# Attention scores made once and kept in SBUF, with a running maximum in place of a pass of its own for the maximum

## The chip, the core and the metric

The kernel runs on one core of a Trainium2 chip. The metric is the device time of one execution in microseconds (us). The core's engines are called as the profile calls them: PE is TensorE, which multiplies matrices (PEld its loading of weights), DVE is VectorE, ACT is ScalarE, POOL is GpSimd, SP is SyncE. PE writes to PSUM only; the other engines here read PSUM or SBUF and write SBUF, and POOL works in SBUF alone.

## What is computed

One decoder layer over x of 32 x 56 x 128: a small LSTM with Gaussian attention weights, then cross-attention to a context of 32 x 1500 x 128 with 16 heads, then a feed-forward stage with 4 experts. The part that the change touches is the cross-attention:

```
q = (Q @ WQ).reshape(N, ql, HEADS, DK)
k = (K @ WK).reshape(N, kl, HEADS, DK)
v = (V @ WV).reshape(N, kl, HEADS, DV)
compat = jnp.einsum('nqhk,nlhk->nhql', q, k) / math.sqrt(DK)
weights = jax.nn.softmax(compat, axis=3)
attn = jnp.einsum('nhqk,nkhv->nqhv', weights, v).reshape(N, ql, HEADS * DV)
return attn @ WO + bO
```

Q is the normalised x, K and V are both the context.

## The kernel before

The weights are folded ahead, WQ with WK and WV with WO, so that per batch element there is one query matrix of 128 x 896 (16 heads x 56 positions), the context itself as key and as value, and one projection per head. The 32 batch elements ("batches") are worked on in 16 pairs. On each engine a function `period(i, k)` writes out one batch, b = 2i + k, as 12 slots; `sequence` writes the first pair, a loop over the middle pairs and the last pair. Nothing but this written order and the semaphores (`need`) sets what runs when.

The context of a batch is cut into 12 chunks of 125 rows. For each chunk:

* **Scores** (PE, `scores`): 125 x 896, in two halves of 448 columns. Context and query are each held as a high and a low part in the type float32r (`ctxT_hi`, `ctxT_lo`, `q_hi`, `q_lo`), and three matmuls per half give hi*hi + hi*lo + lo*hi. Scores go to one of two double banks of PSUM (`score_ps`).
* **Exponential** (ACT, `probs`): reads `score_ps`, writes one of four buffers `probs`.
* **Weighing** (PE, `weigh`): the chunk of the context (`ctx_nat`) times the probabilities, in plain f32, two matmuls of 448 columns (two records each in the profile), summed over the 12 chunks in the PSUM banks `usum_ps`.
* **Sum** (POOL): `prob_sum` += the chunk, 11 additions per batch.

The softmax needs the maximum first. Before a batch's scores are made, PE makes an approximate product the other way round (`side("max")`, 21 matmuls of q_hi x ctxT_hi into 128 x 500), DVE reduces each (`read_max`), builds a diagonal matrix (`max_diag`), PE spreads it over all partitions with two matmuls by ones (`side("spread")`), ACT copies the negative to `neg_max` and ACT writes it into `score_ps` ahead of every chunk (`seed`); the score matmuls add on top of it. All this is done for batch b + 1 beside the work on batch b.

Further work stands in the slots by letters in the table `PLACES` (four places in each slot): t turns a third of the context of batch b + 2 (PE transposes, ACT `turned_hi`, DVE `turned_lo`), q makes a quarter of the next pair's queries (PE, ACT `stage_query`; then ACT `query_hi`, DVE `query_lo`), s takes the sums and p the projections of the pair before (DVE `invert_sums`, `add_heads`). They share two PSUM banks, `SIDE` and `SIDE + 1`: a piece may start once the piece before it in its bank has been read. In the last pair the tokens for the feed-forward stage are normalised, and the experts chosen (`choose_experts`). The feed-forward stage follows, beginning at `hidden(0, 0)`.

Of the kernel before, what the change touches and what calls it, by code (L numbers as in the profile page):

```python
# [18 lines left out]
F32R = mybir.dt.float32r  # L19
# [6 lines left out]
def decoder_layer(nc, x, ctx_1024, W_ih, W_hh, b_ih, b_hh, W_mu, b_mu, W_sig, b_sig,  # L26
# [8 lines left out]
    TOK = 2 * S  # L35
# [17 lines left out]
    NP = 4  # L53
    assert CR * CH == L and RB * 128 == HQ and PAIRS % G4 == 0 and S % U8 == 0

    with ExitStack() as stack:
# [15 lines left out]
        ones_r = sb("ones_r", [128, 128], F32R)  # L72
# [38 lines left out]
        def cut(size, parts=128):  # L111
# [4 lines left out]
        neg_max = [cut(HQ).rearrange("p (a b) -> p a b", a=2) for n in range(2)]  # L116
        cut(3 * HQ)
# [3 lines left out]
        first_sum = q_stage[0:CR, 0]  # L121
# [67 lines left out]
        xT_halves = max_diag[:].rearrange("p (n t) -> p n t", n=2)  # L189
# [6 lines left out]
            "ln_step ln_var rstd_done ln_done xT_ps xT_sb ones_r_made "  # L196
# [5 lines left out]
            "max_ps max_read max_found diag_done spread_ps neg_done seeded scored prob_done "  # L202
# [18 lines left out]
        PLACES = ("m..m mssm ssmm mmpm .mpm mmpm mmpm mqmm mqqt ..dd qt.. t...",  # L221
                  "m..m mm.m mm.m mm.m m.m. m.m. m.mt m.m. m.mt ..dd .... .t..")
# [1308 lines left out]
```

## Time and profile before

| | |
|---|---|
| median of the runs shown | 1717.54 us (1717.15 to 1722.96) |
| the profiled execution | 1721.62 us |
| span of its profile | 1719.5 us |
| LSTM, self-attention, first queries | 0 to 158 us |
| maximum of batch 0 | 158 to 177.6 us |
| cross-attention, 32 batches | 177.6 to 1615.3 us |
| feed-forward stage | 1615.3 to 1719.5 us |
| busy: PE, ACT, DVE, POOL | 96%, 53%, 49%, 46% |

The 14 pairs of the loop repeat each 89.6 us. Records of matmuls overlap, since they are pipelined, so their durations add up to more than the time; what a matmul costs is read from start to start. Durations of the other engines reach about 0.1 us past the start of the next instruction on the same engine for the same reason.

### The profile page before, as it was taken

The page shows a single profiled execution, that of the slowest core. Times are in us where ns is not written, and L with a number is a line of the kernel's source. Part 1 is how long each engine was busy: PE and PEld are TensorE (multiplying, and loading weights), DVE is VectorE, ACT ScalarE, POOL GpSimd, SP SyncE. Part 2 cuts the span into 40 slices and gives each one's busy share as a digit, 9 for nine tenths or more (in the row PEclk, how much of TensorE's full clock was granted, in tenths as well). Part 3 has the DMA queues.
Part 4 walks back from the last instruction along what each step waited for, and adds up shares of the span by engine and source line. Part 5 has one row for each costly group of instructions (what it writes and reads, how often), then busy time and mean ns, then how long its engine had stood idle before and what let it go on. Part 6 is the DMA issues. An engine that isn't in the chain of part 4 may idle for free.

```text
span 1719.5 us, 25064 instructions
## 1 busy us (share of the span) xinstructions
PE 1647.4 (96%) x7783; PEld 1181.7 (69%) x7783; DVE 843.5 (49%) x1772; ACT 918.7 (53%) x1311; POOL 792.1 (46%) x414
## 2 busy tenths in 40 slices
PE   6876999999999999999999999999999999998997
PEld 3344677777777777777777777767677777776664
DVE  3349445454545444454545445454454545454345
ACT  3233565656565656555555556565656565655211
POOL 2003454545454555545455555454545454545410
PEclk9996899999999999999999999999999999999788
DMA  4000000000000000001010101000000000000000
GB/s 150 25 17 2 1 36 37 36 36 36 36 36 36 36 36 36 36 29 43 18 45 15 44 20 40 31 36 36 36 36 36 36 36 36 36 18 1 1 1 22
DMA packets 15052, 54.84 MB, mean 32 GB/s; under 512 B 919, under 2 KB 6122, under 8 KB 15022
## 3 DMA queue, kind: packets, MB, share of 16 engines
q1 hardware_dynamic: 15022, 54.46, 8.4%
q8 instruction: 17, 0.28, 0.1%
q14 instruction: 13, 0.11, 0.0%
HBM read 53.54 MB, written 0.92 MB: 32 GB/s over the span
## 4 chain that ended last, share of the span: by engine, by line
PE 87%; DVE 8%; ACT 2%; issue 1%; POOL 1%; DMA 0%; DVEq 0%; POOLq 0%; ACTq 0%
PE ps L729 32%; PE ps L717 26%; PE ps L598 9%; PE ps L617 3%; PE ps L629 3%; PE ps L779 3%; PE ps L609 3%; PE ps L590 2%; DVE max_diag L1259 2%; PE ps L524 1%; DVE max_parts L1252 1%; PE ps L603 1%; DVE xnorm L1099 1%; ACT arena L877 1%; ACT arena L880 1%
## 5 line engine op out<-in xcount | busy, mean ns | idle before, releaser
L452 POOL TENSOR_TENSOR arena<-arena,probs 125x896 f32<-125x896 f32 x320 | 677.6, 2118 | 546.8 <-ACT probs L1033 456.6
L729 PE MATMUL ps<-probs,ctx_nat 125*128 125x448 f32 x1536 | 685.7, 544 | 0.0
L1252 DVE TENSOR_REDUCE max_parts<-ps 128x1 f32<-128x500 f32 x672 | 451.6, 676 | 354.7 <-PE ps L598 347.2
L1033 ACT ACTIVATE probs<-ps 125x896 f32<-125x896 f32 x384 | 351.6, 916 | 474.3 <-PE ps L717 430.9
L598 PE MATMUL ps<-ctxT_hi,q_hi 128*128 128x500 f32 x672 | 365.1, 544 | 2.2 <-DVE max_parts L1252 1.3
L976 ACT ACTIVATE ps<-arena 125x896 f32<-125x896 f32 x384 | 354.1, 922 | 7.9
L729 PEld LDWEIGHTS ps<-probs,ctx_nat 125*128 125x128 f32 x1536 | 277.6, 191 | 95.8 <-issue 79.7
L717 PE MATMUL ps<-q_hi,ctxT_hi 128*125 128x448 f32 x768 | 331.2, 431 | 1.8 <-ACT ps L976 1.8
L717 PE MATMUL ps<-q_lo,ctxT_hi 128*125 128x448 f32 x768 | 282.8, 368 | 0.0
L717 PE MATMUL ps<-q_hi,ctxT_lo 128*125 128x448 f32 x768 | 281.7, 367 | 0.0
L717 PEld LDWEIGHTS ps<-q_hi,ctxT_hi 128*125 128x125 f32 x768 | 144.5, 188 | 70.0 <-issue 62.1
L598 PEld LDWEIGHTS ps<-ctxT_hi,q_hi 128*128 128x128 f32 x672 | 127.4, 190 | 82.2 <-DVE max_parts L1252 29.7
L717 PEld LDWEIGHTS ps<-q_lo,ctxT_hi 128*125 128x125 f32 x768 | 144.2, 188 | 42.5 <-issue 22.1
L717 PEld LDWEIGHTS ps<-q_hi,ctxT_lo 128*125 128x125 f32 x768 | 143.2, 186 | 14.2
L447 POOL TENSOR_TENSOR arena<-probs 125x896 f32<-125x896 f32 x32 | 68.4, 2139 | 149.0 <-ACT probs L1033 149.0
L1139 DVE TENSOR_TENSOR ctxT_lo<-ps,ctxT_hi 128x500 fp32r<-128x500 f32 x96 | 64.4, 670 | 131.0 <-ACT ctxT_hi L898 131.0
L1244 DVE TENSOR_TENSOR q_lo<-arena,q_hi 128x896 fp32r<-128x896 f32 x32 | 38.8, 1212 | 92.8 <-ACT q_hi L963 92.8
L898 ACT ACTIVATE ctxT_hi<-ps 128x500 fp32r<-128x500 f32 x96 | 56.3, 587 | 45.9 <-PE ps L590 45.9
L617 PEld LDWEIGHTS ps<-vo_w,arena 128*112 128x112 f32 x512 | 64.0, 176 | 23.8 <-issue 23.8
L1290 DVE SCALAR_TENSOR_TENSOR resid<-ps,sum_recip,resid 112x128 f32 (+1 forms) x128 | 44.3, 346 | 63.6 <-PE ps L617 63.6
L629 PEld LDWEIGHTS ps<-xT,qk_w 128*128 128x128 f32 x512 | 67.1, 196 | 11.0 <-issue 9.1
L629 PE MATMUL ps<-xT,qk_w 128*128 (+1 forms) x512 | 69.3, 281 | 0.6 <-ACT xT L859 0.6
(186 smaller groups left out, 1259.6 us busy)
## 6 DMA issues: line engine op xcount, KB each, us to landing
ctx_raw<-in_ctx_dram SPq DMA_DIRECT2D x32, 750.0 KB
ctx_nat<-in_ctx_dram SPq DMA_DIRECT2D x32, 750.0 KB
w_sb<-in_L_ffn_W_dram SPq DMA_DIRECT2D x1, 1024.0 KB
resid<-in_x_dram SPq DMA_DIRECT2D x1, 896.0 KB, 6.7
out_dram<-ctx_raw SPq DMA_DIRECT2D x4, 224.0 KB, 2.5
ctx_raw<-in_L_xattn_WQ_dram SPq DMA_DIRECT2D x1, 512.0 KB
w_sb<-in_L_xattn_WK_dram SPq DMA_DIRECT2D x1, 512.0 KB
w_sb<-in_L_xattn_WV_dram SPq DMA_DIRECT2D x1, 512.0 KB
```

The source lines that it names most:

```text
L447: g.tensor_tensor(first_sum if k == 0 else summed, chunk[0], chunk[1], ALU.add).then_inc(s["prob_added"], 1)
L452: g.tensor_tensor(summed, first_sum if j == 2 and k == 0 else summed, chunk[j % NP], ALU.add).then_inc(s["prob_added"], 1)
L598: mm(ps[:, bank, 0:MC], q_hi[nk][:, block_ * 128:(block_ + 1) * 128], ctxT_hi[nk][:, part * MC:(part + 1) * MC], start=True, stop=True).th ...
L617: m = mm(ps[0:TOK, bank, n * D:(n + 1) * D], u_sum[:, h].rearrange("p b q -> p (b q)"), vo_w[:, h, :], start=True, stop=True)
L629: m = mm(ps[:, bank, n * TOK:(n + 1) * TOK], qk_w[:, 4 * which + n, :], xT[:, bass.ds(i + 1, 1), :].rearrange("p k t -> p (k t)"), start=T ...
L717: m = mm(score_ps[j % 2][:, half, :], cx[k][:, rows], q[k][:, cols], start=False, stop=True, skip_group_check=True)
L729: m = mm(usum_ps[:, half, :], ctx_nat[k][:, j, :], probs[j % NP][:, half, :], start=(j == 0), stop=(j == CH - 1))
L898: a(ctxT_hi[k][:, which * MC:(which + 1) * MC], ps[:, bank, 0:MC], ACT.Copy).then_inc(s["ctxT_hi_done"], 1)
L976: a(score_ps[j % 2], neg_max[k][0:CR], ACT.Copy).then_inc(s["seeded"], 1)
L1033: a(probs[j % NP][:], score_ps[j % 2], ACT.Exp, scale=SCALE).then_inc(s["prob_done"], 1)
L1139: v.tensor_tensor(ctxT_lo[k][:, part], ps[:, bank, 0:MC], ctxT_hi[k][:, part].bitcast(F32), ALU.subtract).then_inc(s["ctxT_lo_done"], 1)
L1252: v.tensor_reduce(max_parts[:, which:which + 1], ps[:, bank, 0:MC], AX.X, ALU.max).then_inc(s["max_read"], 1)
```

## The change

The score matmuls of batch b + 1 now run beside the weighing of batch b. Each chunk of scores is copied out of PSUM by ACT (`keep_scores`) into one of 12 buffers `ring`, and DVE keeps an elementwise maximum over the chunks in `run_max` (`run_maximum`, 11 per batch, each waiting for its chunk; ACT's copy of a chunk waits for the maximum that reads it). When all 12 chunks are there, PE turns `run_max` (`turn_max`, 8 transposes), DVE reduces it over the context (`find_max`), and PE spreads the maximum over the partitions (`spread_max`, 8 small matmuls) into the two side banks. DVE then subtracts it from each chunk in place (`subtract_max`), ACT takes the exponential in place (`exponential`; chunk 0 in two halves), and POOL and PE use the same buffer. Gone are the 21 matmuls and reductions, the diagonal, the spreading by ones, the negative maximum and the 12 seeds. The copy of chunk j of batch b + 1 into `ring[j]` waits for `weigh` and for POOL's addition of chunk j of batch b. The side banks hold the maximum until the last subtraction, so that the pieces t, q, s, p start in slot 6. The queries are made two pairs ahead, and the LSTM, self-attention and feed-forward stages stay as they were, but for the last pair's tokens, now mostly one period earlier.

```diff
-        probs = [sb(f"probs{n}", [CR, 2, HALF]) for n in range(NP)]
+        ring = [cut(HQ, CR).rearrange("p (a b) -> p a b", a=2) for n in range(5)]
...
+        run_max = cut(HQ, CR).rearrange("p (a b) -> p a b", a=2)
+        ring.append(wo_raw[0:CR].rearrange("p f n -> p (f n)")[:, 0:HQ].rearrange("p (a b) -> p a b", a=2))
+        ring += [sb(f"ring{n}", [CR, 2, HALF])[:] for n in range(len(ring), CH)]
...
-        PLACES = ("m..m mssm ssmm mmpm .mpm mmpm mmpm mqmm mqqt ..dd qt.. t...",
-                  "m..m mm.m mm.m mm.m m.m. m.m. m.mt m.m. m.mt ..dd .... .t..")
+        PLACES = (".... .... .... .... .... .... .t.t .t.p .p.p .p.. .... ....",
+                  ".... .... .... .... .... .... .t.t .t.q .q.q .qss ss.. ....")
...
+        EARLY = 4
+        SUBS_AT = {1: (4, 5), 2: (6,), 3: (7, 8), 4: (9,), 5: (10, 11)}
+        EXPS_AT = {0: (2, 3), **SUBS_AT}
...
@@ PE
+                    need(pe, "copied", CH * b + j - 1)
+                    need(pe, "maxed", (CH - 1) * (b - 1) + CH - 2 + j if j < 2 else (CH - 1) * b + j - 2)
...
+            for j in range(CH):
+                for half in range(2):
+                    scores(0, 0, j, half)
...
+                for half in range(2):
+                    turn_max(i, k, half)
+                if not last:
+                    for half in range(2):
+                        scores(b + 1, 1 - k, 0, half)
+                for half in range(2):
+                    spread_max(b, half)
+                if not last:
+                    for half in range(2):
+                        scores(b + 1, 1 - k, 1, half)
                 for j in range(CH):
                     for half in range(2):
+                        weigh(i, b, k, j, half)
                         beside(j, half)
                     for half in range(2):
+                        if 1 <= j < CH - 1 and not last:
+                            scores(b + 1, 1 - k, j + 1, half)
                         beside(j, 2 + half)
...
@@ ACT
+            def keep_scores(b, j):
+
+                need(act, "scored", CH * b + j + 1)
+                need(act, "maxed", (CH - 1) * b + j if j else 0)
+                need(act, "weighted", CH * (b - 1) + j + 1)
+                need(act, "prob_added", (CH - 1) * (b - 1) + max(j, 1))
+                a(ring[j], score_ps[j % 2], ACT.Copy).then_inc(s["copied"], 1)
...
+                if not first:
+                    take_u(i, k)
+                exponential(b, 0)
+                exponential(b, 1)
                 for j in range(CH):
+                    if j:
+                        side_copies(i, k, j - 1)
+                    if not last:
+                        keep_scores(b + 1, j)
+                    for n in EXPS_AT.get(j, ()):
+                        exponential(b, n)
+                    if j == 6 and not (isinstance(i, int) and i == PAIRS - 1):
+                        query_hi(i + 1, k)
...
@@ DVE
+            def run_maximum(b, j):
...
+                v.tensor_tensor(run_max, ring[0] if j == 1 else run_max, score_ps[j % 2], ALU.max).then_inc(s["maxed"], 1)
...
+                    v.tensor_tensor(ring[j][:, part], ring[j][:, part], ps[0:CR, SIDE + part.start:SIDE + part.stop, 0:HALF],
+                                    ALU.subtract).then_inc(s["subbed"], 1)
...
+                for half in range(2):
+                    find_max(b, half)
+                if not first:
+                    take_u(i, k)
+                for j in range(EARLY):
+                    subtract_max(b, j)
+                for j in range(1, CH):
+                    if not (last_pair and k == 1):
+                        run_maximum(b + 1, j)
+                    for n in SUBS_AT.get(j, ()):
+                        subtract_max(b, n)
+                    late_turns(i, k, j - 1)
+                    if j == 6 and not last_pair:
+                        query_lo(i + 1, k)
+                    if last_pair:
+                        beside_last_pair(k, j)
+                    side_reads(i, k, j, range(4))
```

**DVE, a whole period (the first, k = 0; the loop repeats it).** Before: `L1252` is the reduction of the maximum, `L1259` the diagonal, `L1139` the low part of the turned context, `L1244` `query_lo`, `L1267` `take_u`.

```order
L1252 TENSOR_REDUCE max_parts<-ps 128x1 [waits s_max_ps] x20
L1256 TENSOR_REDUCE max_all<-max_parts 128x7 [waits s_diag_done,s_max_read]
L1259 TENSOR_TENSOR max_diag<-ident,max_all 128x896 [waits s_spread_ps,s_max_found]
L1139 TENSOR_TENSOR ctxT_lo<-ps,ctxT_hi 128x500 [waits s_ctxT_hi_done] x2
L1244 TENSOR_TENSOR q_lo<-arena,q_hi 128x896 [waits s_q_hi_done]
```

Now, from the end of one period's reads on into the next (its line numbers are the changed kernel's: `L1270` `find_max`, `L1286` `take_u`, `L1278` a subtraction, `L1264` the running maximum, `L1253` `query_lo`, `L1148` the low part of the turned context):

```order
L1270 TENSOR_REDUCE max_all<-ps 112x4 [waits s_spread_ps,s_run_turned] x2
L1286 COPY arena<-ps 128x8x56 [waits s_weighted]
L1278 TENSOR_TENSOR arena<-arena,ps 125x448 [waits s_spread_ps,s_copied]
L1278 TENSOR_TENSOR arena<-arena,ps 125x448 [waits s_spread_ps]
L1278 TENSOR_TENSOR arena<-arena,ps 125x896 [waits s_spread_ps,s_copied] x3
L1264 TENSOR_TENSOR arena<-arena,ps 125x896 [waits s_run_turned,s_copied,s_scored]
L1278 TENSOR_TENSOR arena<-arena,ps 125x896 [waits s_spread_ps,s_copied]
L1278 TENSOR_TENSOR wo_raw<-wo_raw,ps 125x896 [waits s_spread_ps,s_copied]
L1264 TENSOR_TENSOR arena<-arena,ps 125x896 [waits s_maxed,s_scored]
...
L1253 TENSOR_TENSOR q_lo<-arena,q_hi 128x896 [waits s_q_hi_done]
L1264 TENSOR_TENSOR arena<-arena,ps 125x896 [waits s_maxed,s_scored]
L1148 TENSOR_TENSOR ctxT_lo<-ps,ctxT_hi 128x500 [waits s_ctxT_hi_done] x2
```

Twenty-one short reductions have given way to 11 maxima and 12 subtractions over 896 columns, and `query_lo` and the low parts of the context now stand behind them in DVE's order.

**PE, where one batch passes to the next.** Before, between two chunks (`L717` scores, `L729` weighing, `L598` maximum):

```order
L729 MATMUL ps<-probs,ctx_nat 128x448 [waits s_prob_done]
L729 MATMUL ps<-probs,ctx_nat 128x448
L598 MATMUL ps<-ctxT_hi,q_hi 128x500 [waits s_max_read]
L717 MATMUL ps<-q_hi,ctxT_hi 125x448 [waits s_seeded]
L717 MATMUL ps<-q_lo,ctxT_hi 125x448
L717 MATMUL ps<-q_hi,ctxT_lo 125x448
L598 MATMUL ps<-ctxT_hi,q_hi 128x500 [waits s_max_read]
```

Now (`L703` scores, `L717` `turn_max`, `L725` `spread_max`, `L737` weighing):

```order
L717 MATMUL ps<-ident,arena 112x125 [waits s_ctxT_lo_done]
L717 MATMUL ps<-ident,arena 112x125 x3
L703 MATMUL ps<-q_hi,ctxT_hi 125x448 [waits s_copied,s_maxed,s_ctxT_lo_done,s_q_lo_done]
...
L725 MATMUL ps<-ident_r,max_all 125x112 [waits s_max_found]
L725 MATMUL ps<-ident_r,max_all 125x112 x3
L725 MATMUL ps<-ident_r,max_all 125x112 [waits s_max_found]
L725 MATMUL ps<-ident_r,max_all 125x112 x3
L703 MATMUL ps<-q_hi,ctxT_hi 125x448 [waits s_maxed,s_copied]
...
L737 MATMUL ps<-arena,ctx_nat 128x448 [waits s_nat_in1,s_prob_done,s_u_dve,s_u_act]
L737 MATMUL ps<-arena,ctx_nat 128x448 [waits s_prob_done] x2
```

Only two chunks of scores stand between the running maximum and the first weighing that depends on it.

**ACT, the first copies and exponentials of a period, now** (`L987` `keep_scores`, `L993` `exponential`):

```order
L993 ACTIVATE arena<-arena 125x896 [waits s_subbed]
L987 ACTIVATE arena<-ps 125x896 [waits s_prob_added,s_weighted,s_scored]
L993 ACTIVATE arena<-arena 125x896 [waits s_subbed] x2
L987 ACTIVATE arena<-ps 125x896 [waits s_weighted,s_prob_added,s_maxed,s_scored]
L993 ACTIVATE arena<-arena 125x896 [waits s_subbed]
L993 ACTIVATE wo_raw<-wo_raw 125x896 [waits s_subbed]
```

The copy of the next batch's chunk 0 stands ahead of the exponentials of chunks 2 and 3, and waits for POOL.

## Rows read from the trace of the kernel before

**Rows 1.** The page, part 1: busy us, share of the span and instructions by engine.

```profile
PE 1647.4 (96%) x7783; PEld 1181.7 (69%) x7783; DVE 843.5 (49%) x1772; ACT 918.7 (53%) x1311; POOL 792.1 (46%) x414
```

**Rows 2.** Stretches: length, busy us by engine (count), PE clock share, DMA share, GB/s.

```profile
158.00:177.00 19.00, 14.88 (x29) 6.45 (x27) 16.41 (x25) 3.05 (x6) 4.93 (x1) 0.68 0.00 0
880.40:970.00 89.60, 89.34 (x408) 65.68 (x407) 44.13 (x78) 52.94 (x67) 46.57 (x23) 1.00 0.09 34
1555.70:1615.30 59.60, 50.60 (x190) 32.92 (x189) 24.70 (x47) 27.51 (x35) 37.68 (x22) 0.89 0.00 1
1615.30:1719.50 104.20, 93.46 (x369) 64.76 (x368) 46.58 (x127) 13.35 (x23) 12.63 (x12) 0.84 0.04 9
```

**Rows 3.** PE in order of time: chunks without side work (start, us, what).

```profile
1556.95 1.67 PE L729 MATMUL ps<-probs,ctx_nat 125*128 125x448 f32 x4
...
1559.06 0.37 PE L717 MATMUL ps<-q_hi,ctxT_hi 128*125 128x448 f32 x1
1559.27 0.36 PE L717 MATMUL ps<-q_lo,ctxT_hi 128*125 128x448 f32 x1
...
1562.39 1.67 PE L729 MATMUL ps<-probs,ctx_nat 125*128 125x448 f32 x4
```

**Rows 4.** PE in order of time: a maximum, sums, a projection, turns of the context.

```profile
889.88 0.39 PE L598 MATMUL ps<-ctxT_hi,q_hi 128*128 128x500 f32 x1
890.11 0.36 PE L717 MATMUL ps<-q_hi,ctxT_hi 128*125 128x448 f32 x1
...
893.89 0.86 PE L609 MATMUL ps<-ones,arena 125*112 125x1 f32 x8
894.60 1.00 PE L729 MATMUL ps<-probs,ctx_nat 125*128 125x448 f32 x2
...
904.42 1.04 PE L617 MATMUL ps<-vo_w,arena 128*112 128x128 f32 x8
905.30 0.92 PE L729 MATMUL ps<-probs,ctx_nat 125*128 125x448 f32 x2
...
933.81 0.59 PE L590 MATMUL ps<-ident,ctx_raw 125*128 125x125 f32 x4
934.24 1.67 PE L729 MATMUL ps<-probs,ctx_nat 125*128 125x448 f32 x4
```

**Rows 5.** Instructions grouped by line: busy us, mean ns, idle before them.

```profile
L1252 DVE TENSOR_REDUCE max_parts<-ps 128x1 f32<-128x500 f32 x672 | 451.6, 676 | 354.7 <-PE ps L598 347.2 <-issue 6.2
L1033 ACT ACTIVATE probs<-ps 125x896 f32<-125x896 f32 x384 | 351.6, 916 | 474.3 <-PE ps L717 430.9 <-POOL arena L452 37.7 <-POOL arena L447 5.5
L963 ACT ACTIVATE q_hi<-arena 128x896 fp32r<-128x896 f32 x32 | 30.4, 949 | 0.0
L1139 DVE TENSOR_TENSOR ctxT_lo<-ps,ctxT_hi 128x500 fp32r<-128x500 f32 x96 | 64.4, 670 | 131.0 <-ACT ctxT_hi L898 131.0
```

**Rows 6.** DVE and POOL in order of time: operands in PSUM and in SBUF beside POOL.

```profile
1652.12 5.01 POOL L473 TENSOR_TENSOR resid<-resid,arena 112x512 f32<-112x512 f32 x4 [4.39 <-DVE arena L1481]
...
1654.60 1.09 DVE L1342 TENSOR_TENSOR q_lo<-max_diag,ps 128x896 fp32r<-128x896 f32 x1 [2.56 <-PE ps L581]
...
925.45 1.09 DVE L1259 TENSOR_TENSOR max_diag<-ident,max_all 128x896 fp32r<-128x896 f32 x1
...
879.80 2.21 DVE L1259 TENSOR_TENSOR max_diag<-ident,max_all 128x896 fp32r<-128x896 f32 x1
878.95 2.10 POOL L452 TENSOR_TENSOR arena<-arena,probs 125x896 f32<-125x896 f32 x1 [1.33 <-ACT probs L1033]
900.17 4.29 POOL L452 TENSOR_TENSOR arena<-arena,probs 125x896 f32<-125x896 f32 x2 [5.88 <-PE ps L609]
```

**Rows 7.** DVE in order of time: the last pair's token scaling and choice of experts.

```profile
1566.71 6.43 DVE L1099 TENSOR_SCALAR xnorm<-resid,meanvar,rstd 112x128 f32<-112x128 f32 x8 [0.58 <-POOL rstd L377]
...
1594.10 0.20 DVE L1308 TENSOR_REDUCE arena<-arena 112x12 f32<-112x48 f32 x1
...
1602.53 0.61 DVE L1327 TENSOR_TENSOR max_diag<-xT,max_diag 128x448 fp32r<-128x448 f32 x1
```

More of the change, by code:

```diff
@@ L581, in spread_mask, with turn, sums @@
                 mm(ps[:, mask_bank(e), 0:GT], pick_e[:, e, :], onehotT[n], start=True, stop=True).then_inc(s["mask_ps"], 1)
+            def turn(i, k, which, bank):
+                if which == 0:
+                    need(pe, f"ctx_in{k}", 16 * (i + 2))
+                for c in range(TG):
+                    m = tr(ps[:, bank, c * CR:(c + 1) * CR], ctx_in[k][:, which * TG + c, :], ident[0:CR, 0:CR])
+                m.then_inc(s["ctxT_ps"], 1)
+            def sums(pair, which, bank):
+                if which == 0:
+                    need(pe, "prob_added", (CH - 1) * 2 * (pair + 1))
+                for n in range(4):
+                    m = mm(ps[0:TOK, bank, n:n + 1], prob_sum[:, 4 * which + n].rearrange("p b q -> p (b q)"), ones[0:CR, 0:1], start=True, stop=True)
+                m.then_inc(s["sums_ps"], 1)
@@ L619, in side @@
+                    turn(i, k, which, bank)
+                elif what == "sums":
+                    sums(i, which, bank)
+                elif what == "project":
+                    project(i - 1, which, bank)
+                elif what == "query":
+                    query(i + 2, which, bank)
                 elif what == "tokens":
@@ L626, in side @@
                     spread_mask(0, which)
-                elif what == "query":
-                    for n in range(4):
-                        m = mm(ps[:, bank, n * TOK:(n + 1) * TOK], qk_w[:, 4 * which + n, :],
-                               xT[:, bass.ds(i + 1, 1), :].rearrange("p k t -> p (k t)"), start=True, stop=True)
-                    m.then_inc(s["q_ps"], 1)
             def beside_first(u):
@@ L978, in _, with exponential @@
+            def exponential(b, j):
+                for part in ((slice(0, 1), slice(1, 2)) if j == 0 else (slice(0, 2),)):
+                    need(act, "subbed", step_count(b, j, part.stop - 1))
+                    a(ring[j][:, part], ring[j][:, part], ACT.Exp, scale=SCALE).then_inc(s["prob_done"], 1)
             copy_tokens(TOKEN_BANKS[1], 2, 0)
             for u in range(4):
-                stage_query(-1, u, SIDE + u % 2)
-            query_hi(-1, 0)
+                stage_query(0, u, SIDE + u % 2)
```

353 lines of the change are left out of this document (139 added, 214 removed).

## The prediction, made before the changed kernel was run

> **What bounds the kernel now.** The busy shares come first [rows 1]: PE 96%, no other engine over 53%. A share over the whole span says little of a stage, so the stretches come next [rows 2]: in a pair of the loop, 89.60 us long, PE is busy for 89.34. That could still be a PE that works at somebody's pace, so its work is priced from start to start. A chunk of scores and weighing alone takes 2.72 us (1556.95 to 1562.39 is two) [rows 3]. A maximum takes 0.23, a set of four sums 0.71, a set of four projections 0.88, four turns 0.43 [rows 4]. I take the queries, the same eight records of 128 rows, as a projection. A pair then needs 24 x 2.72 = 65.3 for chunks, 42 x 0.23 = 9.7 for the maximum, 4 x 0.71 + 4 x 0.88 + 4 x 0.88 + 6 x 0.43 = 12.5 for side work and about 0.9 for four spreadings by ones. That is 88.4 of 89.6: PE is the bound in the loop, with 1.2 of gaps. ACT and DVE wait for PE there [rows 5]. The ends differ: ahead of the loop PE is granted 0.68 of its clock on average, between its two levels of 1.2 and 2.4 GHz, and follows DVE's reductions, and the last batch takes 59.6 us because PE waits for tokens and for the choice of experts [rows 2].
>
> **What goes from PE.** Per pair the maximum and the spreading, 9.7 + 0.9 = 10.6. New are 16 turns of the running maximum, at 0.105 each as the turns of the context (0.43 for four) [rows 4], 1.7, and 16 small spreadings. The trace has none of 112 columns in float32r; the nearest rows are 0.09 (eight sums in 0.71) and 0.11 (eight projections in 0.88) [rows 4]. I take 0.10, 1.6 in all. The sixteen cost between 0.8, if they ran at half of that, and 3 if at twice. PE's own work falls to 88.4 - 10.6 + 3.3 = 81.1. If PE stayed the bound with the gaps of before, a pair would take 82.3 and the kernel lose some 110 us. So the question is what is late now.
>
> **What the other engines get.** A subtraction or running maximum reads PSUM and SBUF, 896 columns. The row of that form is 1.09 us, and it ran while POOL was busy [rows 6]; with no wait the next instruction starts about 0.08 earlier, so 1.01 apart. DVE per pair: 22 maxima and 24 subtractions, 46 x 1.01 = 46.5, in place of 42 x 0.6. It has room on average (about 65 of 89), as has ACT, whose copies and exponentials replace exponentials and seeds one for one (0.92 from PSUM, 0.95 from SBUF, 0.85 apart) [rows 5]. POOL keeps its 22 additions, 2.19 apart when back to back (two in 4.29, the second of them 2.10) [rows 6]. No engine is full. But each works in its written order, and there are two places where a chain of them is longer than what PE has in hand.
>
> **The first places, at a batch's start.** Let `turn_max` start at 0. PE: turns to 0.84, scores of chunk 0 (six matmuls 0.205 apart [rows 3], 1.23) to 2.07, spreading to 2.5 and 2.9, scores of chunk 1 to 4.1, weighing of chunk 0 to 5.6. DVE meanwhile: two reductions of 500 columns (0.68 each [rows 5]) to 1.9, `take_u` to 2.4, then from 2.7, when the first spreading has landed, half a subtraction, half, and that of chunk 1, done 4.9. Its exponential is done at 5.9; the handover adds 0.1, and PE, ready at 5.6, waits **0.4**. The next wait is longer. Scores of chunk 2 need their PSUM bank, and ACT's copy of the chunk in it goes to `ring[0]`, which POOL must have added: POOL starts at 6.0 with the exponential of chunk 1, ends at 8.2, the copy ends at 9.1, and PE, ready at 7.5, goes on at 9.25: **1.75**.
>
> **The third, in slot 7.** From 9.15 on DVE has 13 instructions ahead of the running maximum of chunk 6 (five maxima, eight subtractions): 9.15 + 13 x 1.01 = 22.3, done 23.4. Behind it in a row: ACT's copy to 24.3, `query_hi` to 25.2, DVE's `query_lo` to 26.3, the maximum of chunk 7 (1.0), the low part of the first turned third (0.67 [rows 5]), done 28.0. PE has six chunks and two groups of turns, 6 x 2.72 + 2 x 0.43 = 17.2, from 9.25 to 26.45, and then wants the side bank of that third: it waits **1.5**. With k = 0 there is a fourth: the second set of projections needs the bank of the last third, whose low part stands on DVE behind the reading of the first set: four additions of heads (1.1), a maximum (1.0) and itself (0.7), 2.8 to 3.0 with the handovers, against PE's weighing of 1.5: **1.5**.
>
> A pair: 81.1 + 2 x (0.4 + 1.75 + 1.5) + 1.5 = **89.9** us, as before. What PE gave away comes back as four waits.
>
> **The whole.** Before the loop: scoring batch 0 runs at DVE's and ACT's pace. The copy of a chunk waits for its maximum and PE for the copy of two chunks earlier: 1.23, 0.16 from the start of the next matmul to the end of a record of 0.36, 1.09 and 0.92, with handovers 3.6 per two chunks, 21.5 for twelve; the clock is at 0.68 there before [rows 2], so I add 2.5. From 159 the first `turn_max` comes at 183, 5.4 later than the first scores did at 177.6. The first pair has no projections and fewer waits: 85. Then 14 pairs of 89.9 less 2 for queries that pair 14 needn't make: 1256.6. Batch 30 takes over the tokens; two scalings took 6.43 beside POOL [rows 7], three cost DVE about 9: 49. The last batch has no scores to make: 5.6 to the second weighing, and 11 x 1.5. But the choice of experts, 8.4 us before (1594.10 to 1602.53) [rows 7], can start only behind the subtractions at 18 and meets a POOL that is never idle: 28 to 29. Two and a half chunks and the one-hot turns follow, partly at the lower clock: 37. The sum is 183 + 85 + 1256.6 + 49 + 37 = 1610.6, where the feed-forward stage began at 1615.3; it keeps its 104.2 [rows 2]. The span becomes 1714.8, less than 1719.5 by 4.7. The profiled execution was 1721.6, 4.1 over the median of the runs. I set the change against the median: 1717.5 - 4.7 = **1713 us**. My own bounds: gaps of 0 to 2.4 in a pair, dear or cheap spreadings and the ends make it 1690 to 1740.
>
> **Rival 1: `query_lo` just misses POOL's gap, slower.** Its two inputs lie in SBUF. Such an instruction took 1.09 with POOL idle and 2.21 when it started 1.25 us before the end of an addition (879.80 against 878.95 + 2.10) [rows 6]: it waits for the end. The Trainium skill (GPSIMD Engine Reference, Key points) says the two engines share SBUF interfaces, with contention when DVE has two SBUF inputs. The trace agrees, and adds that the wait is for the whole rest. In the new period POOL never pauses. By my times it starts its eighth addition 14.1 after the copy at 9.1, if the first at 1.0, and ends at 16.3; `query_lo` arrives at 16.1. It gets in. If the chain of 13 on DVE is 0.3 later, it waits 2.1 more, each batch: 31 x 2.2 = 68, so **1781**. It decides in 2% of the chain.
>
> **Rival 2: DVE's operations come 1.1 apart, slower.** Each now carries two or three waits; 1.01 is from sequences with one. At 1.10 the third wait grows by 15 x 0.09 = 1.35 a batch, 42 us: **1755**.
>
> **Rival 3: the waits aren't there, faster.** If the copies start earlier than I think (POOL's first addition 1 us sooner, handovers hidden), the second and third waits shrink by 1 each: 31 x 2 = 62, **1651**; without any of the four, 1600. For it: the chains exceed PE's work by 1.5 of 17 only. Against it: each wait is written in the code, and their parts have rows.
>
> **A rule that speaks another way.** The Trainium skill (VectorE: DVE Perf Modes, the errata table) gives 120 + columns cycles for a source in PSUM and 58 + columns from SBUF at 0.96 GHz. By an estimate from that page the new operations would take 1.06 us; the row says 1.09, and by the page the third wait would be 0.4 shorter, 12 us less in all. The row decides.
>
> **Chances.** The forecast's case (89 to 91.5 a pair) 0.50; rival 1, 0.15; rival 2, 0.13; rival 3, 0.22, half of it between 1640 and 1690 and half under 1640. About two in ten lie outside 1640 to 1782: that half, and what is worse than rival 1. A difference under 0.5% (1709 to 1726) a measurement hardly tells from none. The forecast's own range of 1690 to 1740 splits 0.17 faster, 0.18 same, 0.15 slower. With the rivals: faster 0.17 + 0.22 = 0.39, same 0.18 + 0.02 = 0.20, slower 0.41.
>
> **What would show it.** In the trace of the changed kernel: pairs of 89.9 between two `turn_max`; PE busy for about 81 of them; ahead of the scores of chunk 2 an idle of 1.75 that ends with an ACT copy, which itself waited for POOL; in slot 7 one of 1.5 that ends with the low part of the context; `query_lo` at 1.1 to 1.4, or at 3 if rival 1 holds; running maxima 1.01 apart if rival 2 doesn't. I am wrong if the pairs are under 88 with PE never idle for over 0.5, or if PE's clock share in the loop is below 1.

## The result: slower by 0.8%, where 0.3% faster was forecast

| | before | changed |
|---|---|---|
| median of the runs, us | 1717.43 (1717.15 to 1722.96) | 1732.19 (1731.37 to 1734.21) |
| ratio, 95% interval | | 1.008 (1.006 to 1.010) |
| span of the profiled execution (its time) | 1719.5 (1721.6) | 1730.1 (1731.8) |
| a pair of the loop | 89.60 | 90.7 |

The forecast was 1713, a span of 1714.8. The time lies inside the range, but the sign is the other one: the change costs 15 us. The four waits that the prediction names are there; PE's own work beside them had been summed too low, by 0.9 us of 81.1 in each pair.

Page, part 1, of the changed kernel, against [rows 1]:

```profile
PE 1549.0 (90%) x7555; PEld 1089.3 (63%) x7555; DVE 1131.5 (65%) x1868; ACT 895.3 (52%) x1279; POOL 809.9 (47%) x414
```

PE gave away 98 us of busy time and the kernel grew longer. The stretches, against [rows 2] (the scoring of batch 0; a pair; batch 30; the last batch; the feed-forward stage):

```profile
158.00:177.00 19.00, 15.26 (x86) 12.88 (x84) 12.42 (x10) 9.65 (x13) 2.55 (x1) 1.00 0.01 2
903.02:993.73 90.71, 83.60 (x394) 59.97 (x393) 61.73 (x83) 51.45 (x64) 47.80 (x22) 1.00 0.09 34
1536.71:1588.47 51.76, 44.45 (x206) 31.91 (x204) 42.34 (x86) 23.78 (x29) 26.17 (x14) 0.93 0.04 16
1588.47:1623.26 34.79, 26.49 (x80) 13.53 (x78) 25.53 (x29) 16.05 (x21) 27.95 (x15) 0.85 0.00 0
1623.26:1730.10 106.84, 96.12 (x368) 67.30 (x368) 47.49 (x128) 12.80 (x22) 15.88 (x14) 0.82 0.04 9
```

In a pair PE is busy for 83.60 of 90.71, at a full clock share of 1.00: 7.1 us of every pair are idle. That counts each wait short: a record of the weighing is 0.54 long, and unhindered the next starts 0.375 after it, so a wait costs 0.17 more than its bracket says. PE in order of time in the batch that begins at 903.02 (start, us, what; in brackets how long PE was idle before it and what ended that):

```profile
903.02 1.06 PE L717 MATMUL ps<-ident,arena 125*112 125x125 f32 x8
...
907.22 3.52 PE L737 MATMUL ps<-arena,ctx_nat 125*128 125x448 f32 x8
912.15 0.47 PE L703 MATMUL ps<-q_hi,ctxT_hi 128*125 128x448 f32 x1 [1.42 <-ACT arena L987]
...
930.99 0.65 PE L588 MATMUL ps<-ident,ctx_raw 125*128 125x125 f32 x4 [1.35 <-DVE ctxT_lo L1148]
...
936.73 1.13 PE L604 MATMUL ps<-vo_w,arena 128*112 128x128 f32 x8 [1.50 <-DVE ctxT_lo L1148]
...
947.59 1.06 PE L717 MATMUL ps<-ident,arena 125*112 125x125 f32 x8
```

These are the forecast's places: ahead of the scores of chunk 2 (9.13 after `turn_max`, forecast 9.25), in slot 7 (27.97, forecast 28.0), and the second projection (1.50, forecast 1.5). The forecast's small first wait (0.4) has no bracket, but it is there: the eight records of weighing take 3.52, where two sets of four, 1.67 long and 1.50 apart, would take 3.17. What each stands behind, on ACT, POOL and DVE in the same batch:

```profile
911.18 0.92 ACT L987 ACTIVATE arena<-ps 125x896 f32<-125x896 f32 x1 [2.27 <-POOL arena L453]
909.07 2.08 POOL L453 TENSOR_TENSOR arena<-arena 125x896 f32<-125x896 f32 x1 [19.56 <-ACT arena L993]
912.23 1.09 DVE L1264 TENSOR_TENSOR arena<-arena,ps 125x896 f32<-125x896 f32 x1 [2.30 <-ACT arena L987]
...
925.21 1.08 DVE L1264 TENSOR_TENSOR arena<-arena,ps 125x896 f32<-125x896 f32 x1
928.26 1.09 DVE L1253 TENSOR_TENSOR q_lo<-arena,q_hi 128x896 fp32r<-128x896 f32 x1 [1.97 <-ACT q_hi L979]
929.27 1.08 DVE L1264 TENSOR_TENSOR arena<-arena,ps 125x896 f32<-125x896 f32 x1
930.26 1.25 DVE L1148 TENSOR_TENSOR ctxT_lo<-ps,ctxT_hi 128x500 fp32r<-128x500 f32 x2
```

POOL's first addition ends at 911.15 and ACT's copy (L987) starts 0.03 later; with the copy both PE and DVE go on. DVE then runs its chain without a pause from 912.23 to 926.3, waits 1.97 for ACT's `query_hi`, and the low part at 930.26 lets PE into slot 7. In the second batch (947.59) the same two waits are 1.43 and 1.27.

### The profile page after: what moved, and what is told of

Read it like the earlier page. It is cut to its first block and busy times, and to the rows that moved or that the text cites. A ratio compares the mean times of both kernels' runs of the same rounds, so it can differ in the third digit from the quotient of the medians.

```text
span 1730.1 us, 25245 instructions
## 1 busy us (share of the span) xinstructions
PE 1549.0 (90%) x7555; PEld 1089.3 (63%) x7555; DVE 1131.5 (65%) x1868; ACT 895.3 (52%) x1279; POOL 809.9 (47%) x414
## 5 line engine op out<-in xcount | busy, mean ns | idle before, releaser
L453 POOL TENSOR_TENSOR arena<-arena 125x896 f32<-125x896 f32 x128 | 269.6, 2106 | 669.8 <-ACT arena L993 663.9
L1264 DVE TENSOR_TENSOR arena<-arena,ps 125x896 f32<-125x896 f32 x352 | 380.4, 1081 | 188.4 <-PE ps L703 116.9
L453 POOL TENSOR_TENSOR arena<-arena,ring 125x896 f32<-125x896 f32 x192 | 426.3, 2220 | 17.0 <-POOL arena L453 0.5
L703 PE MATMUL ps<-q_hi,ctxT_hi 128*125 128x448 f32 x768 | 348.1, 453 | 48.8 <-ACT arena L987 47.3
L987 ACT ACTIVATE ring<-ps 125x896 f32<-125x896 f32 x192 | 176.3, 918 | 401.8 <-PE ps L737 207.5
L737 PE MATMUL ps<-ring,ctx_nat 125*128 125x448 f32 x768 | 327.2, 546 | 0.0
L703 PE MATMUL ps<-q_hi,ctxT_lo 128*125 128x448 f32 x768 | 281.6, 367 | 0.0
L703 PE MATMUL ps<-q_lo,ctxT_hi 128*125 128x448 f32 x768 | 281.4, 366 | 0.0
L737 PE MATMUL ps<-arena,ctx_nat 125*128 125x448 f32 x640 | 271.2, 547 | 3.4 <-ACT arena L993 1.1
L703 PEld LDWEIGHTS ps<-q_hi,ctxT_hi 128*125 128x125 f32 x768 | 143.4, 187 | 112.0 <-ACT arena L987 72.5
L1278 DVE TENSOR_TENSOR ring<-ring,ps 125x896 f32<-125x896 f32 x192 | 201.5, 1077 | 0.0
L987 ACT ACTIVATE arena<-ps 125x896 f32<-125x896 f32 x160 | 146.5, 916 | 88.1 <-POOL arena L453 70.6
L993 ACT ACTIVATE arena<-arena 125x896 f32<-125x896 f32 (+1 forms) x192 | 153.5, 824 | 71.3 <-DVE arena L1278 71.2
L993 ACT ACTIVATE ring<-ring 125x896 f32<-125x896 f32 x192 | 182.8, 952 | 6.5
L737 PEld LDWEIGHTS ps<-ring,ctx_nat 125*128 125x128 f32 x768 | 136.8, 191 | 70.9 <-issue 68.0
L737 PEld LDWEIGHTS ps<-arena,ctx_nat 125*128 125x128 f32 x640 | 117.8, 190 | 93.8 <-issue 56.9
L1278 DVE TENSOR_TENSOR arena<-arena,ps 125x896 f32<-125x896 f32 (+1 forms) x192 | 167.1, 925 | 8.4 <-PE ps L725 8.4
L703 PEld LDWEIGHTS ps<-q_lo,ctxT_hi 128*125 128x125 f32 x768 | 144.3, 188 | 28.7 <-issue 18.5
L703 PEld LDWEIGHTS ps<-q_hi,ctxT_lo 128*125 128x125 f32 x768 | 142.7, 186 | 14.0
```

Of the source, the lines that this page charges most:

```text
L453: g.tensor_tensor(summed, chunk[0] if j == 1 else summed, chunk[j], ALU.add).then_inc(s["prob_added"], 1)
L703: m = mm(score_ps[j % 2][:, half, :], cx[k][:, rows], q[k][:, cols], start=(n == 0), stop=(n == 2))
L737: m = mm(usum_ps[:, half, :], ctx_nat[k][:, j, :], ring[j][:, half, :], start=(j == 0), stop=(j == CH - 1))
L987: a(ring[j], score_ps[j % 2], ACT.Copy).then_inc(s["copied"], 1)
L993: a(ring[j][:, part], ring[j][:, part], ACT.Exp, scale=SCALE).then_inc(s["prob_done"], 1)
L1264: v.tensor_tensor(run_max, ring[0] if j == 1 else run_max, score_ps[j % 2], ALU.max).then_inc(s["maxed"], 1)
```

## The experiments

Times are medians; "before" is the kernel before in the same group of runs, and the ratio is taken to it. The changed kernel stands at 1.008. It ran in the first group only, and the kernel before moved from 1717.4 to 1723.3 between groups; so a ratio within 0.004 of another settles nothing by itself, and there the length of a pair in the trace decides.

**1. The buffer of chunk 0, and PE's work at two places.** Four runs shared one group (before 1723.25).

`two_first_buffers`:

```diff
+        other = x_halves[0:CR].bitcast(F32).rearrange("p (a b) -> p a b", a=2)
+        def buf(k, j):
+            return other if j == 0 and k == 0 else ring[j]
...
-                need(act, "prob_added", (CH - 1) * (b - 1) + max(j, 1))
-                a(ring[j], score_ps[j % 2], ACT.Copy).then_inc(s["copied"], 1)
+                need(act, "prob_added", (CH - 1) * (b - ago(j)) + max(j, 1))
+                a(buf(k, j), score_ps[j % 2], ACT.Copy).then_inc(s["copied"], 1)
```

(`ago(j)` is 2 for chunk 0 and 1 for the others; each use of `ring[j]` becomes `buf(k, j)`.)

> Chunk 0 of the even batches gets a buffer of its own, so that ACT's copy of the next batch's chunk 0 no longer waits for POOL's first addition. Nothing else is changed. Theory (chains that cross the engines set the period, and PE waits at their ends): ACT is free for that copy at 908.9 instead of 911.18 in the batch that begins at 903.02. PE then loses its wait of 1.42 ahead of the scores of chunk 2, and DVE's first running maximum comes 2.4 earlier, 909.85 for 912.23, and its chain with it, so that the wait of 1.35 in slot 7 falls to about 0.3. That is 2.4 a batch, 31 batches: 1732 - 74 = 1658. If query_lo now meets an addition of POOL in its middle, about 1.1 of it comes back: 1692. I expect 1670, between 1655 and 1692. Rival A (PE's own work, larger than I summed, sets the pair; its waits are only where it runs ahead): within 10 of 1732. Rival B (what the copy waited for is made up at the next wait in the batch): the wait in slot 7 grows from 1.35 to 2.8, within 10 of 1732.

Measured: 1674.7, ratio 0.970 (0.967 to 0.973). The wait of 1.42 is in no batch of the loop any more; that in slot 7 fell from 1.35 to 1.18 and the second projection kept its 1.50:

```profile
879.94 1.06 PE L724 MATMUL ps<-ident,arena 125*112 125x125 f32 x8
906.07 0.65 PE L595 MATMUL ps<-ident,ctx_raw 125*128 125x125 f32 x4 [1.18 <-DVE ctxT_lo L1155]
911.84 1.13 PE L611 MATMUL ps<-vo_w,arena 128*112 128x128 f32 x8 [1.50 <-DVE ctxT_lo L1155]
922.69 1.06 PE L724 MATMUL ps<-ident,arena 125*112 125x125 f32 x8
```

The third turn comes 26.13 after `turn_max` in place of 27.97. That is 1.84 sooner, not 2.4, and since PE comes sooner too, the wait there shrank by 0.17 only; the forecast of 0.3 for it had left that out. A pair takes 86.97. The wait is a real cost, and it is not paid again elsewhere: Rivals A and B fall.

`light_middle` and `light_end` leave out the third of the three matmuls of the scores (for chunks 3 to 5, or 9 to 11):

```diff
-                for n, (cx, q) in enumerate(((ctxT_hi, q_hi), (ctxT_hi, q_lo), (ctxT_lo, q_hi))):
+                parts = ((ctxT_hi, q_hi), (ctxT_hi, q_lo), (ctxT_lo, q_hi))[0:2 if 3 <= j < 6 else 3]
+                for n, (cx, q) in enumerate(parts):
```

> PE's work is made less between its two waits of a batch: the third product of the scores (low part of the context) is left out for chunks 3, 4 and 5, six matmuls of 0.205 a batch, 1.23. The scores of these chunks are a little less exact by it; nothing else is changed. Theory (chains): the third wait ends with DVE's low part of the context, which does not depend on PE's pace there. The wait in slot 7 grows from 1.35 to 2.6 and the time stays, 1732, within 4. Rival A (PE's work sets the pair): 31 x 1.23 less, 1694.

> The same amount of PE's work is left out behind the waits: the third product of the scores for chunks 9, 10 and 11, six matmuls of 0.205 a batch, 1.23. Theory (chains): from the last wait to the next turn_max PE is the one that is waited for, so nearly all of it shows: 31 x 1.1 to 31 x 1.23 less, 1694 to 1698. Rival A (PE's work sets the pair) says 1694 too; with the run that leaves out as much in the middle the two are told apart. Rival C (DVE sets the end of the batch as well, by its heads and maxima): within 6 of 1732.

Measured: 1732.6 (ratio 1.0044, 1.0025 to 1.0063) and 1706.1 (0.989, 0.986 to 0.993). The batch of `light_middle` that begins at 907.10 reaches slot 7 at 935.07, 27.97 later, to the hundredth what it was with six matmuls more:

```profile
935.07 0.65 PE L588 MATMUL ps<-ident,ctx_raw 125*128 125x125 f32 x4 [1.77 <-DVE ctxT_lo L1149]
```

I had expected a wait of 2.6 there; the rest lies in pauses of 0.1 to 0.35 behind three of the weighings. A pair takes 90.72, what it takes with all six. In `light_end` the same work, taken away behind the last wait, makes a pair of 88.3, 2.4 less, nearly all of the 2 x 1.23. The time stays 8 above the forecast's 1694 to 1698: in the profile the first `turn_max` comes 3.5 later than in the changed kernel, at 185.06, and two batches lose 3.3 each to PE's clock (the last section has them). So one engine's work is free at one place of a batch and counts in full at another: PE's up to slot 7 is free, behind it, not.

`double_max5`:

```diff
+                if j == 5:
+                    v.tensor_tensor(run_max, run_max, score_ps[j % 2], ALU.max).then_inc(s["bits_set"], 1)
+                    need(dve, "bits_set", b + 1)
                 v.tensor_tensor(run_max, ring[0] if j == 1 else run_max, score_ps[j % 2], ALU.max).then_inc(s["maxed"], 1)
```

> DVE takes the running maximum of chunk 5 twice, the second time behind the first: one instruction of 1.08 more (1.0 to 1.1 apart) in the chain between the first running maximum and the low part in slot 7. The result is the same. Theory (chains): the wait in slot 7 grows by 1.0 to 1.1 in every batch, 31 x 1.05 and 1 in the scoring of batch 0: 1732 + 33 = 1765, within 5. Rival A (PE's work sets the pair, DVE is busy for 65% of the span and has room): within 5 of 1732.

Measured: 1844.0, ratio 1.069 (1.065 to 1.073). That is 3.5 us a batch for one instruction of 1.08, where 1.05 was expected. The median of `query_lo` went from 1.19 to 2.23: it is the prediction's first rival, met with one instruction more. The next group takes half the dose.

**2. Half the dose, and the other wait.** (before 1719.21)

`half_max5` takes `run_max[:, 0:1]` and `score_ps[j % 2][:, 0:1]` in the extra line.

> As double_max5, but the extra instruction takes the maximum of one half of chunk 5 only, 448 columns, 0.6 of DVE's time in place of 1.05. Theory (the cost of a longer chain comes in steps, at POOL's additions): query_lo starts at 928.26 in the batch of 903.02 and takes 1.09 to 1.19, so it comes within 0.1 to 0.3 of the end of an addition already; in double_max5 it took 2.12 to 2.28. With 0.6 more it misses the same end and waits for the same next one, so the half dose costs as much as the whole: the third turn 30.2 after turn_max as in double_max5 (27.97 in the changed kernel), query_lo at 2.6 to 2.8, and a time within 10 of double_max5's 1844. Rival D (cost in proportion to the added work, the doubled run's rest being the clock alone): query_lo at 1.1 to 1.9, third turn at 28.6, 1732 + 31 x 0.6 = 1751 to 1760.

Measured: 1839.0, ratio 1.069 (1.066 to 1.072): half the work, the whole price. DVE's `query_lo` and low part in `half_max5`, in the batch that begins at 918.25:

```profile
944.04 2.75 DVE L1253 TENSOR_TENSOR q_lo<-arena,q_hi 128x896 fp32r<-128x896 f32 x1 [1.82 <-ACT q_hi L979]
947.71 1.25 DVE L1148 TENSOR_TENSOR ctxT_lo<-ps,ctxT_hi 128x500 fp32r<-128x500 f32 x2
```

The same in `double_max5`, in the batch that begins at 921.67:

```profile
947.91 2.28 DVE L1253 TENSOR_TENSOR q_lo<-arena,q_hi 128x896 fp32r<-128x896 f32 x1 [1.82 <-ACT q_hi L979]
951.11 1.25 DVE L1148 TENSOR_TENSOR ctxT_lo<-ps,ctxT_hi 128x500 fp32r<-128x500 f32 x2
```

It starts 25.79 and 26.24 after `turn_max` and ends 28.54 and 28.52 after it: not the work in front sets its end, but something that stands at the same place in both. In the changed kernel it starts at 25.24 and ends at 26.33. Two of POOL's additions, the third of the last six in the changed kernel and the fourth in `half_max5`:

```profile
926.28 2.11 POOL L453 TENSOR_TENSOR arena<-arena,ring 125x896 f32<-125x896 f32 x1
```
```profile
943.75 2.08 POOL L453 TENSOR_TENSOR arena<-arena,ring 125x896 f32<-125x896 f32 x1
```

The former ends 25.37 after `turn_max`, the latter 27.58. The changed kernel's `query_lo` arrives 0.13 before the end of the one; 0.55 later it has missed it, waits for the end of the other, and in both kernels it ends 0.96 behind the addition's end. The Trainium skill (GPSIMD Engine Reference, Key points) has DVE and POOL contend for SBUF; the trace agrees, and shows the cost as a step.

Rival 1's price was 2.2 a batch, and the third turn is 2.2 later (948.43 - 918.25 = 30.18). The pair went from 90.7 to 98.9, though, 4.1 a batch. The rest lies where PE's clock is low. In `half_max5`, slot 7 of the batch before, and the stretches from there to the next `turn_max`:

```profile
899.33 1.09 PE L588 MATMUL ps<-ident,ctx_raw 125*128 125x125 f32 x4 [3.26 <-DVE ctxT_lo L1148]
```
```profile
899.33:904.50 5.17, 5.17 (x19) 4.88 (x20) 0.53 (x1) 1.04 (x2) 2.40 (x2) 0.50 0.00 0
904.50:918.25 13.75, 12.72 (x58) 8.66 (x58) 9.54 (x22) 2.75 (x3) 0.00 (x0) 0.97 0.00 0
```

After a wait of 3.26 PE is granted 0.50, that is 1.2 GHz, for 5 us; a matmul of 448 columns in float32r starts 0.37 after the one before in place of 0.205. Behind the waits of up to 1.50 in the changed kernel's loop the share stays at 1.00. In `double_max5`, where the wait is 2.8, some batches with k = 0 keep a full clock, and these take 46.8, 2.2 more than in the changed kernel; so the two costs are seen apart.

`query_late` moves `query_hi` and `query_lo` of k = 0 (it ran in the group of part 3, before 1719.56):

```diff
-                    if j == 6 and not last_pair:
+                    if j == (9 if k == 0 else 6) and not last_pair:
```

(in ACT's and in DVE's loop).

> In the first batch of each pair (k = 0) ACT's query_hi and DVE's query_lo are moved from j = 6 to j = 9, behind the copies and the low parts of the context; in the second batch they stay. Theory (chains): in slot 7 of k = 0 the low part of the context comes behind one DVE instruction less and does not wait for ACT's query_hi, at least 1.9 earlier, and PE's wait of 1.35 there is gone; k = 1 keeps its own of 1.3 and the second projection its 1.5. 15 x 1.35 less: 1712, between 1707 and 1718. Rival B (the wait is made up at the next place, the second projection): that wait grows from 1.5 to 2.85, 1732.

Measured: 1727.8, ratio 1.0037 (1.0016 to 1.0059). The wait in slot 7 of k = 0 is gone, and a new one ends the batch:

```profile
944.59 1.06 PE L717 MATMUL ps<-ident,arena 125*112 125x125 f32 x8 [1.12 <-DVE arena L1264]
```

A pair takes 90.6, as in the changed kernel (90.7). Rival B seems to hold, at another place than it named. DVE shows why:

```profile
939.88 1.09 DVE L1253 TENSOR_TENSOR q_lo<-arena,q_hi 128x896 fp32r<-128x896 f32 x1 [1.97 <-ACT q_hi L979]
940.89 0.35 DVE L1309 SCALAR_TENSOR_TENSOR resid<-ps,sum_recip,resid 112x128 f32 x1
...
942.26 2.20 DVE L1264 TENSOR_TENSOR arena<-arena,ps 125x896 f32<-125x896 f32 x2
```

`query_lo` waits 1.97 for ACT and holds up the last heads, and behind them both last maxima, for which `turn_max` waits. `query_last` puts DVE's `query_lo` at j = 11 instead.

> As query_late, but DVE's query_lo of the first batch (k = 0) stands at j = 11, behind the last running maximum; ACT's query_hi stays at j = 9. In query_late PE's wait in slot 7 of k = 0 was gone, but one of 1.12 came ahead of turn_max: query_lo stood in front of the last heads and both last running maxima on DVE. Theory (chains, each placed by what stands behind it): behind the last maximum DVE idles 0.81 for the turned maximum anyway, so query_lo costs 0.1 to 0.3 there and the 1.35 of slot 7 is kept: k = 0 takes 43.3 to 43.6 in place of 44.57, 1732 - 15 x 1.1 = 1716, between 1712 and 1722. Rival B (what is won at one wait is always paid at a later one): 44.4, as in query_late, 1728 to 1732.

Measured: 1711.7, ratio 0.996 (0.994 to 0.998), a pair of 89.70: k = 0 at 43.16, k = 1 at 46.54 (it had 46.13; `query_lo` now holds its start up by 0.4). The move was right, its first place was not.

**3. Places, and all together.** (before 1719.56)

`turns_later`:

```diff
-        PLACES = (".... .... .... .... .... .... .t.t .t.p .p.p .p.. .... ....",
-                  ".... .... .... .... .... .... .t.t .t.q .q.q .qss ss.. ....")
+        PLACES = (".... .... .... .... .... .... .... .t.t .t.. .ppp .p.. ....",
+                  ".... .... .... .... .... .... .... .t.t .t.q .qqq ssss ....")
```

> Only the tables of places are changed: the turns of the context stand one slot later (7 and 8 instead of 6 and 7), the projections in slots 9 and 10, the queries in 8 and 9, the sums in 10. No instruction is added or taken away. Theory (chains): PE asks for the side bank of the third turn 2.72 later, and the low part of the first is done by then; the wait of 1.35 and that of 1.3 are gone, and with three projections in one slot and a third of the context far ahead of them so is that of 1.5. The wait ahead of the scores of chunk 2 (1.42) stays. A pair loses 4.1: 1732 - 15.5 x 4.1 = 1668, between 1662 and 1690, the upper end if the later projections and sums make a wait of their own ahead of turn_max. Rival A (PE's own work sets the pair): 1732.

Measured: 1680.4, ratio 0.977 (0.974 to 0.980). A pair takes 87.0. Two lines of one table, not an instruction more or less, are worth 3%. The turns keep waits of up to 0.8 (6.5 us in 17 places).

`both_moved` is both edits, the table and the buffer.

> The places of turns_later and the second buffer of chunk 0 of two_first_buffers together. Theory (chains): the pair of two_first_buffers, 86.97, still has waits of 1.18, 1.06 and 1.50 in it; without them it is 83.2, which is what I count as PE's own work. 1675 - 15.5 x 3.74 = 1617, between 1608 and 1640. Rival C (with PE's waits gone another chain is next, DVE's at the batch's start or POOL's additions, which take 24 us of 42): a pair not under 85.5, 1650.

Measured: 1623.6, ratio 0.945 (0.941 to 0.949). A pair:

```profile
846.30:929.61 83.31, 82.99 (x393) 60.21 (x393) 62.03 (x83) 50.41 (x64) 47.99 (x22) 1.00 0.09 37
```

83.31 where 83.2 was expected, but that is not all PE's own work. One bracket is left, of 0.16; from start to start there is more. The first two weighings of a batch, and the exponential of chunk 1:

```profile
850.51 1.67 PE L744 MATMUL ps<-x_halves,ctx_nat 125*128 125x448 f32 x4
852.26 1.77 PE L744 MATMUL ps<-arena,ctx_nat 125*128 125x448 f32 x4
851.26 0.95 ACT L1000 ACTIVATE arena<-arena 125x896 f32<-125x896 f32 x1 [0.42 <-DVE arena L1285]
```

The second starts 1.75 behind the first (1.50 elsewhere), right behind the exponential's end at 852.21, and is itself 0.10 longer: the forecast's first wait, 0.35 a batch. In the same way a pair loses 0.34 and 0.09 ahead of its third turns and 0.15 ahead of a `turn_max`. Without these 1.3, PE's own work is 82.0 a pair. Rival C did not come.

`both_early_norm` moves the token norm too: in `beside_last_pair` the moments and scalings of k = 0 go, and in pair 14

```diff
+                    elif isinstance(i, int) and i == PAIRS - 2 and 8 <= j < 11:
+                        (scale if k else moments)(3, j - 8)
```

does them (POOL's powers with them, at 9, 10, 11 of batch 28).

> As both_moved, and the moments, POOL's powers and the scaling of the first three groups of tokens are moved from batch 30 to batches 28 and 29 (their rows of resid are final from pair 11 on). Batch 30 took 51.76 in the changed kernel and 49.78 in two_first_buffers, where its neighbours took 44.70 and 41.35. Theory: DVE is idle for more than half of the time behind slot 7 of an ordinary batch and takes them in unseen, and batch 30 comes down by 4 to 6: 5 less than both_moved, 1612. Rival: PE waits for them in batches 28 and 29 as it did in 30 (the heads of a projection stand behind them on DVE): no change against both_moved.

Measured: 1618.3, ratio 0.940 (0.935 to 0.945); the intervals of the two overlap, so a gain of 5 us is not shown. In the profiles batch 30 fell from 49.71 to 41.88, and batches 28 and 29 rose only from 40.33 and 40.28 to 41.33 and 40.27. The last `turn_max` is at 1471.40 in place of 1477.69, yet the spans are 1613.4 and 1612.8: the feed-forward stage gave it back. Its length goes with its clock. Of `both_moved` (then of the changed kernel, shown above: 106.84 at 0.82; before, [rows 2]: 104.20 at 0.84):

```profile
1512.00:1612.80 100.80, 90.10 (x368) 62.61 (x368) 47.69 (x128) 12.82 (x22) 16.77 (x14) 0.89 0.04 10
```

In `both_early_norm` the share is 0.82 from 1505.00 on, over 108.40 us. Why it is 0.82 in one and 0.89 in the other stays open; I made no run on it.

## Why the prediction went wrong, step by step

- **Four waits in place of PE's work:** right, in place and cause. From start to start, with the 0.10 by which the first matmuls behind the first two waits come slower, a pair holds 0.35 and 1.68 in its first batch and 0.35 and 1.70 in its second (forecast 0.4 and 1.75 each), in slot 7 1.52 and 1.43 (1.5), and 1.66 ahead of the second projection (1.5): 8.7 in all, forecast 8.8.
- **The chain of 13:** right. From 912.23 to the end of the first low part 18.7, forecast 9.15 to 28.0. The maxima and subtractions are 1.00 apart, as taken from [rows 6]: Rival 2 did not come. By an estimate from the Trainium skill (VectorE: DVE Perf Modes, the errata table) one would take 1.06; the group below says 1.08, between the page and the row of 1.09.

```profile
L1264 DVE TENSOR_TENSOR arena<-arena,ps 125x896 f32<-125x896 f32 x352 | 380.4, 1081 | 188.4 <-PE ps L703 116.9
L703 PE MATMUL ps<-q_hi,ctxT_hi 128*125 128x448 f32 x768 | 348.1, 453 | 48.8 <-ACT arena L987 47.3
L987 ACT ACTIVATE arena<-ps 125x896 f32<-125x896 f32 x160 | 146.5, 916 | 88.1 <-POOL arena L453 70.6
L588 PE MATMUL ps<-ident,ctx_raw 125*128 125x125 f32 x384 | 60.0, 280 | 41.5 <-DVE ctxT_lo L1148 41.2
```

- **PE's own work, 81.1 a pair: the step that failed.** It is 82.0: 90.7 less waits of 8.7 in the changed kernel, and 83.3 less 1.3 in `both_moved`, two readings that agree. The mechanism was right; this term of the sum was 0.9 too small. By the traces some 0.35 of it are the four sets of sums. The prediction priced a set at 0.71, from its start to the next start; but the matmul behind it then follows late, as its own [rows 4] show (the weighing at 894.60 takes 1.00 for two records, the one at 905.30 takes 0.92), so that a set costs 0.80. The small spreadings are another 0.15 (a batch's eight take 0.82, and the scores behind them 0.05 more), the turns of the running maximum 0.1; what is left, 0.3, is spread over the other turns, the queries and the chunks. The price of 88.4 for the work of before lacks the same 0.35, so part of the 1.2 called gaps there was work. No run takes the sums or the spreadings out, so the shares are read from the traces and not tested.
- **No price for a change of kind as such.** Behind transposes the first matmul of the scores is followed 0.285 later in place of 0.205, but it has itself started 0.03 behind the last transpose in place of 0.107. The two cancel; behind the sums, and in small part behind the spreadings, they do not.
- **Where that error could cost anything.** Up to slot 7 nothing: 27.97 against 28.0, since the chain on DVE ends it, and `light_middle` shows that PE's work is free there. All of it lies behind: a pair less its two stretches up to slot 7 is 90.71 - 27.97 - 27.94 = 34.8, where the forecast had 89.9 - 56.0 = 33.9. Of these 0.9, some 0.7 are PE's work and 0.2 the wait of the second projection. `light_end` shows that behind slot 7 PE's work counts in full.
- **The whole:** first `turn_max` 181.56 (forecast 183), first pair 86.33 (85), pairs 1 to 14 1268.8 (1256.6), batch 30 51.76 (49), last batch 34.79 (37), feed-forward stage 106.84 (104.2). The differences, -1.4, +1.3, +12.2, +2.8, -2.2 and +2.6, make +15.3: 1730.1 for 1714.8. The loop is 12 of them; the feed-forward stage's 2.6 goes with its clock, 0.82 for 0.84. That the ends came out near the forecast owes something to luck: the first `turn_max` came at 182.6, 188.4 and 189.2 in `light_middle`, `two_first_buffers` and `turns_later`, with the same code ahead of it.
- **Batch 30:** PE waits 5.24 ahead of the tokens' first transposes, for heads that stand on DVE behind the first group's four scalings; these take 5.62 beside POOL, the next groups' 1.11 each. The forecast had about 9 for three groups; they take 7.8, but most of it falls on the first, behind which PE waits. With all of it moved away (`both_early_norm`) the batch takes 41.88.

```profile
1574.55 1.01 PE L495 MATMUL ps<-ident,xnorm 112*128 112x112 f32 x4 [5.24 <-DVE odd_heads L1307]
1567.83 5.62 DVE L1108 TENSOR_SCALAR xnorm<-resid,meanvar,rstd 112x128 f32<-112x128 f32 x4
```

- **Rival 1** did not come in the changed kernel (`query_lo` 1.09 to 1.24 in the loop), but by less than 0.6 us, as `half_max5` shows; the mechanism is as described, and its price was set too low, 2.2 a batch for 3.5 to 4, since PE's clock falls behind most of the longer waits.
- **Rival 3** (waits not there) is what `both_moved` makes: its 1624 is in the reach of the 1600 to 1651 given.
- **The sign** hung on 0.9 us of 90. Even the forecast's pair was longer than before (89.9 for 89.6); its gain of 4.7 us came from the ends, which move by more than that with the clock (the feed-forward stage took 100.8 to 108.4). A forecast of "as before, 89.9" is not a forecast of faster; chances of 0.39 and 0.41 said so, the single number did not.

## What to carry to other kernels

Where an engine waits at the ends of chains that others walk, split its period at the waits: its work ahead of a wait is free, its work behind the last one counts in full, and only there does an error of the sum show. Price a short piece of work up to where the engine is back in its pace, not to the next start alone, and measure a wait in the same way, from start to start: else part of the work is taken for gaps, or a wait for work. And when a change has made a bound engine light and the time stays, look for the two or three places where it asks too early: one buffer and two lines of a table turned +0.8% into -5.5% here (`both_moved`).

## What was not expected of the hardware

- A DVE instruction with both inputs in SBUF costs beside a busy POOL in steps: 0.6 or 1.05 us more in front of it, the same 2.2 us later. It ended 0.96 behind the end of the addition that it met, whether it arrived 0.13 or 1.8 ahead of it.
- From the second pair on PE's clock share fell to 0.50 behind all 26 waits of 3.2 to 3.3 us in `half_max5` and behind 20 of 26 waits of 2.8 to 2.9 in `double_max5`, and stayed at 1.00 behind waits of 1.5. The length of the wait does not settle it alone: in the changed kernel it fell behind one of 1.88 (1520.53) and not behind one of 1.97 (210.1), and in `double_max5` not behind one of 3.25 (1582.7).
- It also fell where PE had no wait at all. In `both_moved` batch 27 took 44.66 in place of 43.1, and its weighing at 1344.25 took twice its time, right behind the sums (matmuls of one column), with PE busy throughout:

```profile
1343.46 0.92 PE L602 MATMUL ps<-ones,arena 125*112 125x1 f32 x8
1344.25 3.33 PE L744 MATMUL ps<-ring,ctx_nat 125*128 125x448 f32 x4
```

The batches with such a fall (one of 31 there, two in `both_early_norm`, two in `light_end`) are all of those with the sums. It costs 1.6 to 3.3 us each time, in no regular order; the runs don't tell its cause.
